# Key chunks of 128 instead of 125, other places in memory for TensorE's operands, and a rearranged hand-over from attention to experts

## The reference, cut to what matters

```python
# x (8, 224, 512), ctx (8, 750, 512), mask (8, 1, 224, 750), 16 heads of 32, 8 experts of width 2048
Q, K, V = proj(layernorm(x), W_q), proj(ctx, W_k), proj(ctx, W_v)
Q, K = rope(Q), rope(K)
scores = where(mask == 0, -inf, Q @ K.T / sqrt(32))
x = x + tanh(g_xattn) * (softmax(scores) @ V) @ W_o.T
h = layernorm(x); affinity = softmax(h @ gate_w.T).T          # (8, 8 experts, 224)
gating, idx = top_k(affinity, 56)                              # each expert picks 56 rows of each batch
x_in = h[idx]
x_e = (silu(x_in @ w_gate.T) * (x_in @ w_up.T)) @ w_down.T
x = x + tanh(g_ffn) * zeros.at[idx].add(gating * x_e)
```

## The kernel before

| operand | before | after |
|---|---|---|
| `project_context`: weights `w_hi`, `w_lo` | 0 | 0 |
| `c_hi`, `c_lo` at the columns of `keys` | 32, 96, 32, 96 in the first half, 0, 64, 0, 64 in the second | 64 |
| `c_hi`, `c_lo` at the chunks of `values` | 32 + 64 c + 500 k | 64 |
| `experts`: `w_hi`, `w_lo` | 64 | 0 |
| `xs_hi`, `xs_lo` | 0 | 64 |
| `h_hi` / `h_lo` | 64 / 0 | 64 / 64 |
| `e_t` / V in `attend`'s `values` | 64 / 0 | 0 / 0 |
| `wq_sb` / `xT` in the query projection | 0 / 64 | 0 / 0 |

## Time and profile before

### The profile page before, as it was taken

The page is one execution under the profiler, slowest core; times in us unless marked ns, Lnnn a source line. Parts: engine busy times, 40 slices in busy tenths (PEclk is TensorE's granted clock), DMA queues, the critical chain, the costliest instruction groups (busy, mean ns, idle before and its releaser), DMA issues.

```text
span 1834.4 us, 28481 instructions
## 1 busy us (share of the span) xinstructions
PE 1740.8 (95%) x10502; PEld 1545.1 (84%) x10502; DVE 1038.9 (57%) x1786; ACT 839.2 (46%) x1482; POOL 235.4 (13%) x302
## 2 busy tenths in 40 slices
PE   7999999899999999983999999999999999999995
PEld 6898998677777877753999999999999999999995
DVE  6666667777887787754544535435445354453541
ACT  3223225777776877742433434424344243343430
POOL 0000002131231232122000102002020020010101
PEclk9999999999999999995999999999999999999998
DMA  6544547756755755523333535335343252353421
GB/s 242 224 173 186 189 156 220 182 126 153 178 147 135 183 150 134 141 87 96 115 104 103 150 109 143 103 103 151 106 121 127 106 149 104 101 150 109 124 92 20
DMA packets 76301, 251.90 MB, mean 137 GB/s; under 512 B 10784, under 2 KB 10784, under 8 KB 74928
## 3 DMA queue, kind: packets, MB, share of 16 engines
q1 hardware_dynamic: 64208, 216.55, 38.3%
q0 software_dynamic: 12000, 34.12, 7.9%
HBM read 188.01 MB, written 51.61 MB: 131 GB/s over the span
## 4 chain that ended last, share of the span: by engine, by line
PE 52%; POOL 1%; DVE 0%; issue 0%; DMA 0%; DVEq 0%; ACT 0%; POOLq 0%
PE gu_ps L1624 11%; PE gu_ps L1623 11%; PE gu_ps L1622 11%; PE y_ps L1641 6%; PE y_ps L1640 6%; PE y_ps L1639 6%; PE y_ps L1650 1%; PE gu_ps L1608 1%; POOL out L1482 0%; DMA xg<-xn_rows,gather_i 0%; POOL gather_i L1469 0%; POOL xg L1472 0%; DVE xs_lo L1557 0%; DVE y_cols L1584 0%; PE gu_ps L1668 0%
## 5 line engine op out<-in xcount | busy, mean ns | idle before, releaser
L1622 PE MATMUL gu_ps<-xs_hi,ws_hi 128*128 128x448 f32 x1024 | 370.3, 362 | 3.0 <-DVE xs_lo L1557 3.0
L1624 PE MATMUL gu_ps<-xs_hi,ws_lo 128*128 128x448 f32 x1024 | 371.9, 363 | 0.0
L1623 PE MATMUL gu_ps<-xs_lo,ws_hi 128*128 128x448 f32 x1024 | 371.8, 363 | 0.0
L1552 DVE TENSOR_TENSOR ws_lo<-w_raw,ws_hi 128x1024 fp32r<-128x1024 f32 x192 | 235.2, 1226 | 189.3 <-ACT ws_hi L1502 188.3
L1502 ACT ACTIVATE ws_hi<-w_raw 128x1024 fp32r<-128x1024 f32 x192 | 201.5, 1051 | 163.7 <-PE y_ps L1641 150.6
L1298 PEld LDWEIGHTS t_ps<-cst,sm 112*125 112x125 f32 x1536 | 205.0, 190 | 68.6 <-issue 29.3
L990 DVE CUSTOM_DVE_ANT_0 sm<-m_ps,mq 112x752 f32<-112x752 f32 x256 | 229.7, 935 | 34.2 <-PE m_ps L1282 33.8
L1298 PE MATMUL t_ps<-cst,sm 112*125 112x112 f32 x1536 | 233.3, 281 | 15.0 <-DVE e_t L998 11.3
L880 ACT ACTIVATE sm<-sm,least 112x752 f32<-112x752 f32 x256 | 234.7, 919 | 13.7 <-DVE least L990 12.7
L1622 PEld LDWEIGHTS gu_ps<-xs_hi,ws_hi 128*128 128x128 f32 x1024 | 192.0, 187 | 16.9 <-issue 3.3
L1623 PEld LDWEIGHTS gu_ps<-xs_lo,ws_hi 128*128 128x128 f32 x1024 | 192.7, 188 | 14.6
(11 more groups left out here) (153 smaller groups left out, 2438.6 us busy)
## 6 DMA issues: line engine op xcount, KB each, us to landing
w_raw<-wstream SPq DMA_DIRECT2D x192, 512.0 KB, 3.5
ks<-k_split SPq DMA_DIRECT2D x192, 188.0 KB, 5.4
k_split<-k_split SPq DMA_DIRECT2D x32, 752.0 KB, 3.4
v_rows<-v_out SPq DMA_DIRECT2D x16, 750.0 KB
vs<-v_rows SPq DMA_DIRECT2D x16, 750.0 KB
c_raw<-ctxT SPq DMA_DIRECT2D x7, 1500.0 KB, 13.0
qs<-q_hi POOLq DMA_DIRECT2D x64, 112.0 KB, 5.1
mq_raw<-maskq SPq DMA_DIRECT2D x7, 656.2 KB, 10.9
```

What stands on the lines that cost most here:

```text
L1552: nc.vector.tensor_tensor(w_lo[s][:], w_raw[s][:], w_hi[s][:], ALU.subtract).then_inc(wlo_done[s], 1)
L1622: nc.tensor.matmul(o, w_hi[s][:, w], xs_hi[:, c], start=(c == 0), stop=False)
L1623: nc.tensor.matmul(o, w_hi[s][:, w], xs_lo[:, c], start=False, stop=False)
L1624: mm = nc.tensor.matmul(o, w_lo[s][:, w], xs_hi[:, c], start=False, stop=(c == DC - 1))
```

## The change

Keys now lie in two halves of 384 places with 376 keys and 8 zeros each (`SK` = 768), and chunks are 128 wide (`KP` = 128). The elementwise work still goes over 376 of each half where it can (`halves`), and over 768 in three of VectorE's steps and one of ScalarE's for each group of keys. GpSimd zeroes the gaps of `c_hi`, `c_lo`, `k_cos`, `k_rot` at the start, and those of `sm` at the start of `attend`. The host pads the context to 752 and lays out the rotations to match. Tiles are put elsewhere (the table above); units 0 to 3 of `w_hi` and `w_lo` now have their place during the end of `attend`. There ScalarE splits units 0 to 2 after `copy_parts`, and VectorE makes `w_lo` of unit 0 after `norm_2`, of 1 and 2 after L1177. In `experts`, VectorE makes `gather_i` itself, ahead of `gate_t`; each gather has a semaphore of its own, PE transposes gather by gather, SyncE's next weight loads wait for the gathers, and `gate_up` waits for `xs_lo` chunk by chunk.

```diff
-KP, KC = 125, S2 // 125
 KN = 376
-SK = 2 * KN
+S2P = 2 * KN
+KP, KC = P, 6
+HALF = KC // 2 * KP
+SK = 2 * HALF
...
+LINE = 32
+TOP_EDGE, MID_EDGE = 16, 16
+BEFORE = 2 * (B // 2) * D + DC * SLOTS + 2 * SLOTS
+FIRST = BEFORE + 3 * LINE
...
+def halves(row):
+    return row.rearrange("p (a n) -> p a n", a=2)[:, :, 0:KN]
...
-                sb(late, "below", [P, IC * SLOTS - E_OVER * (KC // 2) * PAIR])
-                w_raw = [sb(late, f"w_raw{j}", [P, UNIT]) for j in range(NRAW)]
+                sb(late, "below", [P, FIRST - E_OVER * (KC // 2) * PAIR])
+                first = First(
+                    w_raw=[sb(late, f"w_raw{j}", [P, UNIT]) for j in range(NRAW)],
+                    w_hi=[sb(late, f"ws_hi{j}", [P, UNIT], F32R) for j in range(NRAW)],
+                    w_lo=[sb(late, f"ws_lo{j}", [P, UNIT], F32R) for j in range(NRAW)],
...
+        sb(st, "ctx_line", [P, LINE // 2])
+        c_hi = [sb(st, f"c_hi{j}", [P, DC, SK], F32R) for j in range(2)]
+        c_lo = [sb(st, f"c_lo{j}", [P, DC, SK], F32R) for j in range(2)]
...
-                    nc.gpsimd.memset(c_hi[j][:, :, S2:SK].bitcast(F32), 0.0)
-                    nc.gpsimd.memset(c_lo[j][:, :, S2:SK].bitcast(F32), 0.0).then_inc(pads_set, 1)
+                    for t in (c_hi[j], c_lo[j]):
+                        nc.gpsimd.memset(t[:].rearrange("p c (a n) -> p (c a) n", a=2)[:, :, KN:HALF].bitcast(F32), 0.0)
+                    for t in (k_cos[j], k_rot[j]):
+                        ins = nc.gpsimd.memset(t[:].rearrange("p (a n) -> p a n", a=2)[:, :, KN:HALF], 0.0)
+                    ins.then_inc(pads_set, 1)
...
-                        cols = slice(n * KN, n * KN + KN)
+                        cols = slice(n * HALF, n * HALF + KN)
...
-                    nc.scalar.activation(rows, rows, ACT.Exp, bias=least[:, h % KSLOTS, qc:qc + 1], scale=-1.0,
+                    nc.scalar.activation(halves(rows), halves(rows), ACT.Exp, bias=least[:, h % KSLOTS, qc:qc + 1], scale=-1.0,
...
                 def end():
                     copy_parts(B - 1, NG - 1)
+                    for u in range(LEAD):
+                        act.wait_ge(first.w_in[u], 16)
+                        nc.scalar.activation(first.w_hi[u][:], first.w_raw[u][:], ACT.Copy).then_inc(first.whi_done, 1)
                     x2_columns(B - 1, 0)
...
+                def low_w(u):
+                    dve.wait_ge(first.whi_done, u + 1)
+                    nc.vector.tensor_tensor(first.w_lo[u][:], first.w_raw[u][:], first.w_hi[u][:], ALU.subtract).then_inc(first.wlo_done[u], 1)
...
                     norm_2(b)
+                    low_w(0)
                     dve.wait_ge(rest_made, R_USES * b + R_XNT + 2)
                     nc.vector.tensor_copy(xT[:, 1], m_ps[1][:, 1, 0:2 * S]).then_inc(rest_free, 1)
+                    low_w(1)
+                    low_w(2)
                     logits(b)
...
-                                              ks[:, h % KSLOTS, n * KN:n * KN + KN], start=True, stop=True)
+                                              ks[:, h % KSLOTS, n * HALF:n * HALF + KN], start=True, stop=True)
...
+                for g in range(RG):
+                    hold(gathered[g], 16)
                 for u in range(NRAW, NU):
                     load(0, u)
...
                 dve.wait_ge(turned, 1)
+                nc.vector.tensor_copy(gather_i, gu_ps[0][0:RP, RG * E:2 * RG * E].rearrange("p (g e) -> p g e", g=RG)[:, :, 0:1]
+                                      .rearrange("p g o -> p (g o)")).then_inc(gidx_done, 1)
...
-                for u in range(LEAD):
-                    split_w(0, u)
                 split_x(0)
...
                 def turn_rows(e):
-                    pe.wait_ge(gathered, 16 * RG * (e + 1))
-                    for c in range(DC):
-                        for g in range(RG):
+                    for g in range(RG):
+                        pe.wait_ge(gathered[g], 16 * (e + 1))
+                        for c in range(DC):
...
-                    if u == 0:
-                        pe.wait_ge(xlo_done, DC * (e + 1))
...
+                            if u == 0 and k == 0:
+                                pe.wait_ge(xlo_done, DC * e + c + 1)
```

More of the change, by code:

```diff
@@ L70 @@
 F_XT, F_Q, F_USES = 0, 2, 4
+@dataclass
+class First:
+    w_raw: object
+    w_hi: object
+    w_lo: object
+    w_in: object
+    whi_done: object
+    wlo_done: object
 @dataclass
@@ L139, in program @@
         gains = sb(top, "gains", [P, 2])
-        w_in = [sem(f"w_in{j}") for j in range(NRAW)]
+        sb(top, "top_edge", [P, TOP_EDGE])
         with ExitStack() as mid:
@@ L186, in project_context @@
         cos, sin = rot[:, 0], rot[:, 1]
-        c_hi = [sb(st, f"c_hi{j}", [P, DC, SK], F32R) for j in range(2)]
-        c_lo = [sb(st, f"c_lo{j}", [P, DC, SK], F32R) for j in range(2)]
         k_cos = [sb(st, f"k_cos{j}", [P, SK]) for j in range(2)]
@@ L605, in attend @@
 def attend(nc, sem, sb, ps, both, x, maskq, wo, gatew, kd, vd, xn_rows, out, cst, ident,
-           cos, sin, gains, gate_all, row_all, wstream, w_raw, w_in):
+           cos, sin, gains, gate_all, row_all, wstream, first):
     with ExitStack() as st:
@@ L617, in attend @@
         sm = sb(st, "sm", [QP, SR, QC, SK])
+        e_t = [sb(st, f"e_t{j}", [KP, KC // 2, PAIR]) for j in range(E_OVER, 2 * HG)] + both.e_t
         least, sums = sb(st, "least", [QP, KSLOTS, QC]), sb(st, "sums", [QP, 2, QC, HG])
         parts, spread = sb(st, "parts", [QP, 2, QC * HG]), sb(st, "spread", [QP, 2, QC, P])
-        e_t = [sb(st, f"e_t{j}", [KP, KC // 2, PAIR]) for j in range(E_OVER, 2 * HG)] + both.e_t
         c_r, cx = sb(st, "c_r", [P, S]), sb(st, "cx", [P, NG, S])
@@ L1330, in start @@
                             scores(0, h, qc)
+                    pe.wait_ge(edges_set, 1)
                 def body(b, j, first, last):
@@ L1395, in _, with experts @@
                 every_batch(start, body, end)
[L1398 removed]
+def experts(nc, sem, sb, ps, first, wstream, xn_rows, out_rows, cst, ident, gains, gate_all, row_all):
     with ExitStack() as st:
[L1401 to L1404 removed]
+        xg, y_sb = sb(st, "xg", [RP, RG, D]), sb(st, "y_sb", [RP, RG, D])
+        y_cols = sb(st, "y_cols", [P, DC, SLOTS])
+        silu = [sb(st, f"silu{j}", [P, SLOTS]) for j in range(2)]
         gate_t = sb(st, "gate_t", [RP, E, RG])
         idx_t = sb(st, "idx_t", [RP, E, RG], U32)
[L1407 to L1408 removed]
+        both_i = sb(st, "both_i", [RP, LINE], U32)
+        gather_i, scatter_i = both_i[:, 0:RG], both_i[:, LINE // 2:LINE // 2 + RG]
+        sb(st, "first_place", [P, 3 * NRAW, UNIT])
+        w_raw, w_hi, w_lo = first.w_raw, first.w_hi, first.w_lo
+        sb(st, "half_line", [P, LINE // 2])
         xs_hi, xs_lo = sb(st, "xs_hi", [P, DC, SLOTS], F32R), sb(st, "xs_lo", [P, DC, SLOTS], F32R)
[L1410 removed]
         hid = [sb(st, f"hid{j}", [P, SLOTS]) for j in range(2)]
[L1412 to L1414 removed]
+        h_hi, h_lo = sb(st, "h_hi", [P, IC, SLOTS], F32R), sb(st, "h_lo", [P, IC, SLOTS], F32R)
         gu_ps = [ps(st, f"gu_ps{j}", [P, 512]) for j in range(4)]
         y_ps = [ps(st, f"y_ps{j}", [P, 512]) for j in range(RG)]
[L1420 removed]
+        w_in, whi_done, wlo_done = first.w_in, first.whi_done, first.wlo_done
         w_used = sem("w_used")
@@ L1423, in experts @@
         gidx_done, sidx_done = sem("gidx_done"), sem("sidx_done")
-        gathered, x_turned, xhi_done, xlo_done = sem("gathered"), sem("x_turned"), sem("xhi_done"), sem("xlo_done")
+        gathered, x_turned, xhi_done, xlo_done = [sem(f"gathered{g}") for g in range(RG)], sem("x_turned"), sem("xhi_done"), sem("xlo_done")
         silu_done, hid_done = sem("silu_done"), [sem(f"hid_done{j}") for j in range(2)]
@@ L1695 @@
     sign = np.where(np.arange(DK) < DK // 2, f(-1), f(1))[:, None]
-    rotations = np.zeros((P, 2, SK), f)
-    rotations[:, 0, 0:S2] = np.tile(np.cos(angles), (P // DK, 1))
-    rotations[:, 1, 0:S2] = np.tile(np.sin(angles) * sign, (P // DK, 1))
+    rotations = np.zeros((P, 2, 2, HALF), f)
+    for n in range(2):
+        keys = slice(n * KN, min(n * KN + KN, S2))
+        width = keys.stop - keys.start
+        rotations[:, 0, n, 0:width] = np.tile(np.cos(angles)[:, keys], (P // DK, 1))
+        rotations[:, 1, n, 0:width] = np.tile((np.sin(angles) * sign)[:, keys], (P // DK, 1))
+    rotations = rotations.reshape(P, 2, SK)
     consts[:, C_COS:C_SIN + S] = rotations[:, :, 0:S].reshape(P, 2 * S)
```

65 lines of the change are left out of this document (29 added, 36 removed).

## The result

The changed kernel takes **1807.42 us** (median of 4 runs, 1806.67 to 1807.81), the kernel before took 1837.8 us beside it (4 runs, 1836.28 to 1838.93). The ratio is 0.9835, with a 95% interval of 0.9818 to 0.9852. Forecast were 1808.5 us and a range of 1800 to 1821. The profiled execution took 1807.75 us with a span of 1806.0, so the two spans are 28.4 us apart and the two medians 30.4; a single execution of each can't account for the 2 us between.

The account below looks back on a forecast made before the run. PE's own instruction stream was taken to limit all three blocks, with PE waiting for gathered rows between attention and experts. 5.8 + 1.6 + 3.0 + 12 + 7.0 = 29.4 us off gave 1808.5 us, range 1800 to 1821.

Parts of the forecast that it names:

- Down at the pace of gate-up: Experts: with operands 64 bytes apart, down matmuls go from 203.7 to 200.0 ns; 5.8 us off, bounds 0 and 5.8.
- Keys: Projections: the matmuls of keys go from a mean of 172.1 to 170.0 ns for all 768; 1.6 us off.
- Values: Projections: the 576 matmuls of values get quicker with operands 64 apart and 128 stationary columns; 3.0 us off, bounds 0 and 3.2.
- The attention: Attention transposes: 128 stationary columns take 96 ns, 125 take 109; 14.8 us, four fifths kept after PE's waits, 12 us off.
- Rival A: Attention transposes: 128-column loads are no quicker and take 111.6 ns, adding 3 us where 12 were taken off; 1823.5 us, chance 0.05.
- rival C: Attention: PE is ahead sooner and waits for emptied tiles, so only 3 of 12 us arrive; 1817.5 us, chance 0.12.
- VectorE behind GpSimd's `x2o`: Attention's end: VectorE's moved `w_lo` subtractions stand behind GpSimd's `x2o` and end later; 0 to 1.7 us lost, 0.7 taken.
- The hand-over: Attention to experts: earlier gathers and chunk-wise waiting bring the first expert matmul 7.7 us forward; 7.0 left, bounds 5 and 7.7.
- Gate-up unchanged: Experts: gate-up stays 64 bytes apart with roles swapped, so its units stay 4.80 us apart; 0 us off.
- Rival D: Experts: the new placing, weights at 0 under streams from 64, is slower than the old; 1825.7 us at down's pace, chance 0.04.

Follow-up runs that it names:

- x_same: Changed kernel without the 64-byte spacer before the experts' moving operands, so weights and moving operands both start at 0 modulo 128 bytes; 1829.98 us, ratio 0.9945.
- x_quarter: Changed kernel with a 32-byte spacer in place of 64 before the experts' moving operands, weights at 0 modulo 128 bytes; 1835.15 us, ratio 0.9973.
- c_same: Changed kernel without the spacer before the context's tiles in the projections, so context and weights both start at 0 modulo 128 bytes; 1807.53 us, ratio 0.9826.
- v448: Changed kernel with 448 in place of 512 columns moving in 11 of 12 matmuls of each values group, result incomplete; 1792.25 us.
- wv pair: Two kernels: the changed kernel with V's weights moved to 64 or to 80 modulo 128 bytes, context kept at 64; 1806.3 and 1807.53 us.
- t125: Changed kernel with only the first 125 keys of each 128-wide chunk transposed, copied and multiplied with V, result incomplete; 1820.01 us, ratio 0.9891.
- w_late: Changed kernel with the weight splits of units 0 to 2 back at the experts' start, gather_i still on VectorE; 1811.89 us, ratio 0.9847.
- g_pool: Changed kernel with gather_i copied by GpSimd again, the splits of units 0 to 2 left in the attention's end; 1808.53 us, ratio 0.9834.
- warm: Changed kernel with 21 matmuls nobody reads, run on PE while it waits for the gathers; 1803.98 us, ratio 0.9805.

## Why the prediction was right, point by point

- **Down at the pace of gate-up, 5.8 us:** right. 203.7 became 200.0 ns, 3.65 x 1536 = 5.6 us, and x_same and x_quarter show that the place does it. The reading of the old placing was incomplete: it gave `h_hi` as being where the weights are and left out `h_lo`, which was 64 apart and no quicker.
- **Keys, 1.6 us:** right in kind. 172.0 became 170.6, not 170.0: 1.1 us. c_same gives 1.9 us back.
- **Values, 3.0 us: this step failed.** It took 226.7 ns, the line through the paces of 376 and 448 columns of streams that move from the context or from `xs`, and put it on 512 columns with the roles exchanged. No run shows the 3.0 us: measured are 233.0 ns, and these matmuls got 0.9 x 576 = 0.5 us slower. The pace was not wrong for 512 columns, as two chunks in six of c_same show with 226.7 ns; the place was. 64 apart, the quick place for 376 and 448 columns, is a slow one here, and with the operands there the excess grows with the length, 2.2 ns at 448 columns and 6.3 at 512 (v448). The wv pair, at 231.2 and 231.7 ns for c_same's 229.4, shows that it is not the distance alone. What the quickest place is for all six chunks stays open.
- **The attention, 12 us, bounds 0 and 20:** right that the column count does it, as t125 shows by itself; the term is a little small. The stretch fell by 15.1 us, of which t125 gives 13.3 to the column count; 1.8 are the wait and the clock in the second batch, which no term foresaw. In the 13.3 two errors partly cancel. From t125 to the changed kernel the intervals that begin with a transpose fall from 190.5 to 172.2 us, 143 ns a head and not 116: in the head shown, the interval behind the values fell from 197 to 152 ns, where "perhaps 11" was taken, and those before another kind of instruction, taken at 0, by 13 or 14. And the waits kept a good quarter of these 18.3 us, not a fifth. Other plain fp32 matmuls of the trace before come every 190.6 ns with 224 moving columns and every 429.6 with 512: 239.0 / 288 = 0.83 ns a column, twice the 0.418 given under c_same. From the 96 ns of 112 columns to the 190.6 of 224 it is 94.6 / 112 = 0.84. Rival A fell by the earlier trace rows and by the trace after; rival C, which had only 3 us arrive, fell as well. The reason given, that the wide loads are the quick ones, is too narrow: 120 is as quick, 96 ns. That it is the load at all was the author's assumption; the runs show the column count and not what lies behind it. What holds 125 back stays open.
- **VectorE behind GpSimd's `x2o`, 0.7 us:** didn't come. The row after shows the subtractions at their usual 1.2 us each and GpSimd longer by 1.2 us, under the slack of the rounds. In w_late, without the subtractions, `x2o` is back at 3.12. In this place GpSimd waited and VectorE did not.
- **The hand-over, 7.0 us:** right in its steps, and in this trace a little lucky. Forecast were the first gather 1.9 us behind the gates, the fourth at 5.8, the last four transposes at 9.5, the first expert matmul at 11.7; the trace has 2.0, 5.9, 9.2 and 11.6. In the nine other kernels without idle matmuls and with the splits moved, it is 11.7 to 13.2, as the gathers land, so the changed kernel's trace is the quickest of ten. Its 7.8 us of gain would be 6.2 to 7.7 in theirs. g_pool and w_late show that for the gathers the splits, not the copy, were what had to go, and w_late that over half of the gain, 4.4 us, comes with the splits left where they were.
- **What the sum left out:** the clock at the start of the experts. Before, nine intervals went at the slow pace, from 860.47 on; after, sixteen. (6.07 - 16 x 0.20) - (3.35 - 9 x 0.20) = 1.3 us are lost, which is why experts gained 4.3 us and not 5.6. warm wins it back, and more. The other kernels whose first gathered rows land later have fewer slow intervals, so gates to end varies less (962.3 to 963.5) than the hand-over alone.
- **Gate-up unchanged:** right, 200.0 ns in both. Rival D fell, though the sign of its warning was sound: at a distance of 32 bytes the same block is 28 us slower than at 64.

The total came out within 1.1 us, and part of that is luck. By the stretches of the two traces, 5.2 us of what was forecast did not come (3.2 in the projections, where `values` alone fell 3.5 short, 1.5 in the experts, 0.5 at start and end), and 4.3 came that were not forecast (3.1 between first and last scores, 1.1 behind them, 0.1 in the hand-over). That leaves 28.5 us for 29.4. The medians are 30.4 us apart, on the other side of the forecast, and no trace shows where those last 2 us lie.
